# Both weight buffers of the experts and three of the four score stacks of the first attention in one memory

## The chip, the cores and the metric

The kernel runs on one core of a Trainium2 chip, as one launch. The metric is the device time of that launch in microseconds (us); lower is better. The core has five engines that run side by side and meet only at semaphores: TensorE (PE; its weight loads are shown apart as PEld), VectorE (DVE), ScalarE (ACT), GpSimd (POOL) and SyncE (SP), which issues nearly all DMA transfers. All tiles that the engines compute on lie in SBUF, 128 partitions wide; a tile's start is a byte address that is the same in every partition.

## The reference, cut to what matters

Two transformer layers on x of shape [16, 512, 256]. Layer 0: windowed attention with rotary positions, then a mixture of 8 experts of which each token takes 2. Layer 1: causal attention with xpos positions, then a product with a ternary weight.

```python
x = x + _L0_attn_ref(_layernorm(x), Wqkv, Wout)                  # 16 heads of 16, window 128
x = x + _L0_ffn_ref(_layernorm(x), Wr, br, Wl1, bl1, Wl2, bl2, biases_N)
x = x + _L1_attn_ref(_layernorm(x), Wq, bq, Wk, bk, Wv, bv, Wo, bo)   # causal
x = x + _L1_ffn_ref(_layernorm(x), weight)                       # ternary weight

# _L0_ffn_ref, per token: softmax over 8 scores, top 2, and
h = x @ Wl1[e] + bl1[e]            # 256 -> 2 * 512, both halves
y = (silu(h[:512]) * h[512:]) @ Wl2[e] + bl2[e]                  # 512 -> 256
# weighted sum of the two experts' y
```

## The kernel before, in words

The program has three stages, one after the other, with a barrier of all engines between them: `pipeline` for the first attention (its tiles show as `a_...` in the profile), `experts` (tiles `e_...`), and `pipeline` again for the second attention with the ternary product (`a_...` once more).

**pipeline** goes over the 16 sequences in turns. In turn i, PE makes the transposed scores of sequence i (step `T`, L1203, with a mask product L1080 behind them), ACT takes their exponentials (L672), PE multiplies them with the values (`PV`, L1221), and in the same turn PE makes the scores of sequence i+1 (step `S`, L1177) from which DVE takes each row's maximum (L941 in the first attention, L936 and L941 in the second). Sequence i+2 is projected and rotated (L1075, DVE L921 and L925, POOL L569 to L580), split into three bf16 parts, stored to DRAM (`store`, L473) and read back as stacks (`stack`, L483): `qst` and `kst`, each 98 partitions by 16 heads by 512 positions in bf16, 16,384 bytes in a partition. 96 of the partitions are the parts; the last two hold the negated maximum for q (L488) and ones for k (L440). There are two slots of each stack: sequence s uses `qst[s % 2]` and `kst[s % 2]`. The order of all steps is one list that every engine walks (`order`, sorted by position numbers in `turn`); semaphores are placed by hand, and no planner or pool decides anything. A stack's group g of slot s % 2 is written when the `T` steps of sequence s-2 with that group are done (wait on `t_done` ahead of L483).

**experts** goes over 39 steps: 32 of 512 rows and 7 of 256 rows. A step multiplies gathered rows with one expert's first weights (L1539, 48 matmuls), gates them on ACT and DVE, and multiplies with its second weights (L1555). Even steps use weight slot 0 and odd steps slot 1. A slot is `NW` = 3,072 fp32 columns twice (a rounded part and a rest), so 24,576 bytes in a partition; SP loads it in two transfers (L1380 of 2 MB, L1385 of 1 MB), two biases behind them (L1388, L1389). The weights of step 0 are loaded at the end of the first attention (`first_weights`, L1323) once all `T` steps of sequence 14, the last in slot 0, are done; those of step 1 are loaded in the experts' stage, behind the barrier (L1380).

**SBUF.** Tiles lie one behind the other in the order in which they are made. What `experts` makes ahead of its call of `pipeline` stays through the first attention; what it makes after the call takes the place of the attention's own tiles. `under` (L1313 of the code, `e_under` in the profile) is such a tile that stays: its bytes hold `qst[0]` and `kst[0]` of the first attention, and afterwards weight slot 0. `qst1` and `kst1` are tiles of the first attention, and weight slot 1 (`w1`, `e_w` in the profile) is a tile of the experts alone. The second attention has all four stacks as tiles of its own.

```python
under = sb("under", [P, H * T])                                      # L1313, ahead of the first attention
w = [under[:, 0:2 * NW].rearrange("p (l n) -> p l n", l=2)]          # L1314
w.append(sb("w1", [P, 2, NW]))                                       # L1334, behind it
```

Of the kernel before, what the change touches and what calls it, by code (L numbers as in the profile page):

```python
# [13 lines left out]
BF16 = mybir.dt.bfloat16  # L14
# [5 lines left out]
B, T, D = 16, 512, 256  # L20
P = 128
NT = T // P
KC = D // P
H, DH = 16, 16
# [14 lines left out]
AUG = ROWS + 2  # L39
# [90 lines left out]
def pipeline(nc, name, x_in, x_out, w_all, w_out, tables, biases, window, scale, consts, routed, mixed, ternary_w):  # L130
# [123 lines left out]
    with ctx:  # L254
        def sb(n, shape, dt=F32):
            return ctx.enter_context(nc.sbuf_tensor(f"{name}_{n}", shape, dt))
# [21 lines left out]
        ident = sb("ident", [P, P])  # L278
# [20 lines left out]
        parts = sb("parts", [P, 2, 3, 2, T], BF16)  # L299
        if routed:  # L300
            under = routed[-1][-1]
            qst, kst = ([under[0:AUG, a * H * T // 2:(a + 1) * H * T // 2].bitcast(BF16)
                         .rearrange("p (h t) -> p h t", h=H)] for a in range(2))
            qst.append(sb("qst1", [AUG, H, T], BF16))
            kst.append(sb("kst1", [AUG, H, T], BF16))
        else:
            qst = [sb(f"qst{i}", [AUG, H, T], BF16) for i in range(2)]
            kst = [sb(f"kst{i}", [AUG, H, T], BF16) for i in range(2)]
# [12 lines left out]
        if routed:  # L321
            xs, wr_d, br_d, bn_d, below_d, before_d, choice, ws_d, w1_d, w2_d, starts_d, kept = routed
            gate, place, expert, taken = choice
            rn, row, tile_tab, per_expert, shifts, scattered, padded, first_weights, under = kept
# [935 lines left out]
NW = KC * 2 * FF + FC * D  # L1260
# [27 lines left out]
def experts(nc, xs, ys, w1_d, b1_d, w2_d, b2_d, starts_d, ident_d, choice, yrow):  # L1288
# [10 lines left out]
    with ctx:  # L1299
        def sb(n, shape, dt=F32):  # L1300
            return ctx.enter_context(nc.sbuf_tensor(f"e_{n}", shape, dt))

        def sem(n):
            return ctx.enter_context(nc.semaphore(f"e_{n}"))
# [5 lines left out]
        shifts = sb("shifts", [P, 4, NE])  # L1310
        scattered = [sem(f"scattered{i}") for i in range(2)]
        padded = sem("padded")
        under = sb("under", [P, H * T])  # L1313
        w = [under[:, 0:2 * NW].rearrange("p (l n) -> p l n", l=2)]  # L1314
        b1 = [sb(f"b1{i}", [P, 2 * FC]) for i in range(2)]
        b2 = [sb(f"b2{i}", [P, D]) for i in range(2)]
        w1_loaded = [sem(f"w1_loaded{i}") for i in range(2)]
# [4 lines left out]
        def first_weights(sp, e):  # L1322
# [3 lines left out]
            sp.dma_start(b2[0][:, :], b2_d[e].partition_broadcast(P)).then_inc(b_loaded[0], 16)  # L1326

        pipeline(nc, *held["attention"], held["routed"] +
                 (ws_d, w1_d, w2_d, starts_d, (rn, row, tab, rows, shifts, scattered, padded, first_weights, under)), None, None)

        bank = [ctx.enter_context(nc.psum_tensor(f"e_bank{i}", [P, 512], F32)) for i in range(8)]
        AB, BB, YB, TB = bank[0:2], bank[2:4], bank[4:6], bank[6:8]
        ident = sb("ident", [P, P])
        w.append(sb("w1", [P, 2, NW]))  # L1334
        xg = sb("xg", [P, NT, D])
        xh = [sb(f"xh{i}", [P, KC, T], F32R) for i in range(2)]
        xl = [sb(f"xl{i}", [P, KC, T], F32R) for i in range(2)]
# [255 lines left out]
def ternary(nc, x_in, x_out, w_d, ident_d):  # L1593

    name, _, _, w_all, w_out, tables, biases, window, scale, consts = held["attention"]
    x1, ys = held["mixed"]
    pipeline(nc, name, x1, x_out, w_all, w_out, tables, biases, window, scale, consts, None,
             (ys,) + held["choice"], w_d)
# [105 lines left out]
```

How the kernel before makes its waits and increments, by code:

```python
        @block.sync  # L428
        def _(sp):
            if mixed:
                sp.dma_start(yrow[:, :, :], yrow_d).then_inc(index_loaded, 16)
                sp.dma_start(gate[:, :, :], gate_d).then_inc(index_loaded, 16)
            sp.dma_start(xt[0][:, :, :], x_in[0].rearrange("(t p) d -> p t d", p=P)).then_inc(x_loaded[0], 16)
            sp.dma_start(w_raw, w_all).then_inc(w_loaded, 16)
            sp.dma_start(ident[:, :], ident_d).then_inc(ident_loaded, 16)
            for dst, src in loads:
                sp.dma_start(dst, src).then_inc(const_loaded, 16)
            sp.wait_ge(ones_done, 1)
            for i in range(2):
                sp.dma_start(kst[i][ROWS:AUG, :, :], junk[0:2 * H, 0, :]).then_inc(ones_loaded, 16)
            for st in order:
                if st[0] == "fetch":
                    j = st[1]
                    e, c = divmod(j, NW // WCOLS)
                    src = w1_d[e][:, c, :] if c < KC else w2_d[e].rearrange("p c n -> p (c n)")
                    sp.wait_ge(ws_stored, 16 * j)
                    sp.dma_start(ws[:, 1, :], src).then_inc(ws_loaded, 16)
                elif st[0] == "keep":
                    j = st[1]
                    e, c = divmod(j, NW // WCOLS)
                    sp.wait_ge(rest_done, j + 1)
                    sp.dma_start(ws_d[e][:, :, c * WCOLS:(c + 1) * WCOLS], ws[:, :, :]).then_inc(ws_stored, 16)
                elif st[0] == "pads":
                    sp.wait_ge(counted_rows, 1)
```

## Time and profile before

| | before |
|---|---|
| median of 3 runs | 2888.07 us (2873.35, 2892.66, 2888.07) |
| the profiled execution | 2870.61 us, of it 2868.7 us from the first to the last instruction |
| PE busy | 2463.0 us, 86% of the span |
| DVE / ACT / POOL busy | 1714.3 / 1350.0 / 923.1 us |
| mean granted clock of TensorE | 0.943 of full speed |
| DMA | 490.19 MB, 171 GB/s over the span |

The page has one execution of the program: busy time by engine, the span in 40 slices, the DMA queues, the chain of work that ended last, and the costliest groups of instructions by line and tile. A group's row ends with the idle time of the engine ahead of it and with what ended that idle time. Names of tiles come without buffer numbers: `a_qst` is `qst1` in the first attention and both slots in the second.

### The profile page before, as it was taken

What the parts mean: (1) busy time and instruction counts of PE and PEld (TensorE: products, weight loads), DVE (VectorE), ACT (ScalarE), POOL (GpSimd) and SP (SyncE); (2) the same over time, 40 slices, a digit from 0 to 9 for tenths busy, and PEclk for the clock granted to TensorE, in tenths of its full rate; (3) what the DMA queues carried; (4) which work ended last, traced back from release to release, by engine and by line L of the source; (5) the groups of instructions that cost most, each with busy time, mean ns of one, the idle gap of its engine ahead of it and who ended that gap; (6) DMA issues with size and microseconds to landing.
All of it is one profiled execution on the core that took longest, in us unless ns stands there. A gap on an engine that the chain in (4) does not pass through costs nothing. (4 is left out here: it accounts for less than half of the span.)

```text
span 2868.7 us, 50929 instructions
## 1 busy us (share of the span) xinstructions
PE 2463.0 (86%) x17722; PEld 1682.5 (59%) x17722; DVE 1714.3 (60%) x5759; ACT 1350.0 (47%) x2419; POOL 923.1 (32%) x863
## 2 busy tenths in 40 slices
PE   3788888888889849999999982799999999998997
PEld 2455555555555528898998872455555555555553
DVE  3666676766667535444444434667676677666651
ACT  2455555555555423333333321255655555555654
POOL 2434555444553220000000015344443434444300
PEclk7899999999999969999999996799999999999998
DMA  4456555666545267877777745444455444444320
GB/s 134 152 185 212 185 181 183 205 213 190 176 156 170 75 205 250 285 267 263 267 280 265 252 146 173 119 119 143 127 146 145 134 119 118 124 135 141 117 62 15
DMA packets 259617, 490.19 MB, mean 171 GB/s; under 512 B 25609, under 2 KB 191113, under 8 KB 249417
## 3 DMA queue, kind: packets, MB, share of 16 engines
q1 hardware_dynamic: 241944, 435.23, 48.3%
q0 software_dynamic: 17456, 52.19, 5.4%
q8 instruction: 123, 2.02, 0.3%
q14 instruction: 94, 0.76, 0.1%
HBM read 299.65 MB, written 186.52 MB: 169 GB/s over the span
## 5 line engine op out<-in xcount | busy, mean ns | idle before, releaser
L672 ACT ACTIVATE a_pr<-a_bank 128x512 f32<-128x512 f32 (+1 forms) x1152 | 638.2, 573 | 571.2 <-PE a_bank L1080 500.6
L941 DVE CUSTOM_DVE_ANT_0 a_junk<-a_bank,a_smask 128x256 bf16<-128x256 f32 (+3 forms) x1536 | 652.1, 463 | 375.2 <-PE a_bank L1177 358.1
L1177 PE MATMUL a_bank<-a_kst,a_qst 96*128 96x256 bf16 (+3 forms) x1536 | 354.5, 297 | 76.5 <-DVE a_nmax L941 26.6
L1203 PE MATMUL a_bank<-a_qst,a_kst 98*128 98x256 bf16 (+3 forms) x1536 | 345.0, 292 | 43.0 <-ACT a_pr L672 25.2
L1221 PE MATMUL a_bank<-a_pr,a_va 128*32 128x256 f32 (+3 forms) x4096 | 350.7, 418 | 28.1 <-ACT a_pr L672 25.3
L1080 PE MATMUL a_bank<-a_mask,a_identb 128*128 128x512 bf16 (+2 forms) x1152 | 351.5, 305 | 0.0
L1177 PEld LDWEIGHTS a_bank<-a_kst,a_qst 96*128 96x128 bf16 x1536 | 127.5, 99 | 268.7 <-issue 84.1
L1426 POOL DMA_DIRECT2D results_dram<-e_yt x39 | 29.3, 751 | 619.2 <-DVE e_yt L1494 601.6
L1449 ACT ACTIVATE e_sa<-e_bank,e_b 128x512 f32<-128x512 f32 (+1 forms) x156 | 101.5, 651 | 255.9 <-PE e_bank L1539 236.0
L550 POOL DMA_INDIRECT xs<-e_rn,e_row x128 | 127.1, 993 | 294.8 <-DMA a_kst<-a_parts_dram 89.0
L1203 PEld LDWEIGHTS a_bank<-a_qst,a_kst 98*128 98x128 bf16 x1536 | 134.0, 99 | 143.7 <-ACT a_pr L672 72.9
L1506 DVE SCALAR_TENSOR_TENSOR e_gf<-e_bank,e_b,e_sa 128x512 f32<-128x512 f32 (+1 forms) x156 | 109.4, 701 | 164.8 <-ACT e_sa L1449 164.4
L1539 PE MATMUL e_bank<-e_xh,e_under 128*128 128x512 f32 x640 | 202.1, 397 | 1.4 <-DVE e_xl L1515 1.4
L936 DVE TENSOR_REDUCE a_nmax<-a_bank 128x2 f32<-128x512 f32 (+1 forms) x192 | 129.9, 684 | 97.1 <-PE a_bank L1080 97.1
L1221 PEld LDWEIGHTS a_bank<-a_pr,a_va 128*32 128x32 f32 x4096 | 85.7, 110 | 166.9 <-issue 108.4
L580 POOL TENSOR_TENSOR a_parts<-a_qk,a_parts 128x1024 bf16<-128x1024 f32 x64 | 136.6, 2134 | 80.5 <-ACT a_parts L647 80.4
L1510 DVE TENSOR_TENSOR e_gl<-e_gf,e_gh 128x512 fp32r<-128x512 f32 (+1 forms) x156 | 100.5, 644 | 103.5 <-ACT e_gh L1454 103.5
L1539 PE MATMUL e_bank<-e_xh,e_w 128*128 128x512 f32 (+1 forms) x608 | 161.1, 353 | 0.0
L1454 ACT CAST e_gh<-e_gf 128x512 fp32r<-128x512 f32 (+1 forms) x156 | 90.8, 582 | 142.0 <-DVE e_gf L1506 142.0
L576 POOL TENSOR_TENSOR a_qk<-a_qk,a_parts 128x1024 f32<-128x1024 f32 x64 | 136.7, 2136 | 39.8 <-ACT a_parts L644 39.5
L560 POOL DMA_INDIRECT a_yg<-results_dram,a_yrow x124 | 120.5, 972 | 73.4 <-DVE a_xt L779 45.2
L569 POOL TENSOR_TENSOR a_qk<-a_rt 128x512 f32<-128x512 f32 x64 | 81.8, 1279 | 178.1 <-DVE a_rt L921 115.5
(214 smaller groups left out, 5352.9 us busy)
## 6 DMA issues: line engine op xcount, KB each, us to landing
a_parts_dram<-a_parts SPq DMA_DIRECT2D x224, 256.0 KB
e_under<-ws_dram SPq DMA_DIRECT2D x20, 2048.0 KB, 9.0
e_w<-ws_dram SPq DMA_DIRECT2D x19, 2048.0 KB, 9.2
a_qst<-a_parts_dram SPq DMA_DIRECT2D x96, 384.0 KB, 7.6
a_kst<-a_parts_dram SPq DMA_DIRECT2D x96, 384.0 KB, 8.7
a_parts_dram<-a_parts SPq DMA_DIRECT2D x32, 768.0 KB
e_under<-a_parts_dram SPq DMA_DIRECT2D x64, 384.0 KB, 8.3
ws_dram<-a_ws SPq DMA_DIRECT2D x24, 1024.0 KB, 7.7
```

The lines of the kernel that those rows point to most:

```text
L550: pool.indirect_dma_start(xs, bass.IndirectOffsetOnAxis(ap=row[r % 2][:, k, t:t + 1], axis=0), rn[r % 2][:, t, :], None).then_inc(scattere ...
L560: pool.indirect_dma_start((xn if ahead else yg)[:, t, :], None, ys, bass.IndirectOffsetOnAxis(ap=yrow[:, k, m * NT + t:m * NT + t + 1], ax ...
L576: nc.gpsimd.tensor_tensor(qk[:, a], qk[:, a], parts[:, a, 0], ALU.subtract)\
L580: nc.gpsimd.tensor_tensor(parts[:, a, 2], qk[:, a], parts[:, a, 1], ALU.subtract)\
L672: nc.scalar.activation(pr[b][:, h:h + per, :], TB_[at % 2][:, 0:per * w].rearrange("p (h w) -> p h w", h=per), ACT.Exp, scale=scale).then_ ...
L936: last = nc.vector.tensor_reduce(nmax[:, qb, g * HG + h:g * HG + h + per], SB_[at % 2][:, 0:per * w].rearrange("p (h w) -> p h w", h=per), ...
L941: last = nc.vector.tensor_tensor_reduce(junk[:, at % 2, j * w:(j + 1) * w], SB_[at % 2][:, j * w:(j + 1) * w], smask[:, T - w:T], scale=-1 ...
L1080: return nc.tensor.matmul(out, identb[:, :], rhs, start=False, stop=True, skip_group_check=True)
L1177: last = nc.tensor.matmul(out[:, j * w:(j + 1) * w], q[0:ROWS, hh, qb * P:(qb + 1) * P], k[0:ROWS, hh, k0:k0 + w], start=not whole or j == ...
L1203: nc.tensor.matmul(out[:, j * w:(j + 1) * w], k[0:AUG, hh, b * P:(b + 1) * P], q[0:AUG, hh, q0:q0 + w], start=(j == 0), stop=False, skip_g ...
L1221: last = nc.tensor.matmul(PVB[32 * j:32 * (j + 1), q0:q0 + w], va[i % 2][:, b, (g * HG + j) * VW:(g * HG + j) * VW + 32], pr[b][:, j, :], ...
L1539: last = nc.tensor.matmul(out[:, 0:s.columns], first(s.slot, low)[:, kc, col:col + P], x[s.slot][:, kc, 0:s.columns], start=(p == 0), stop ...
```

## The change

`under` grows from 8,192 to 12,288 fp32 columns. Weight slot 1 becomes its second half and is no tile of its own any more. In the first attention `qst[1]` becomes the third 16,384 bytes of `under`; `kst[1]` stays a tile. The experts' `ident` tile is made ahead of `under` instead of behind the attention. The second attention is not touched.

```diff
         if routed:
             under = routed[-1][-1]
-            qst, kst = ([under[0:AUG, a * H * T // 2:(a + 1) * H * T // 2].bitcast(BF16)
-                         .rearrange("p (h t) -> p h t", h=H)] for a in range(2))
-            qst.append(sb("qst1", [AUG, H, T], BF16))
-            kst.append(sb("kst1", [AUG, H, T], BF16))
+            parts_of = [under[0:AUG, n * H * T // 2:(n + 1) * H * T // 2].bitcast(BF16)
+                        .rearrange("p (h t) -> p h t", h=H) for n in range(3)]
+            qst = [parts_of[0], parts_of[2]]
+            kst = [parts_of[1], sb("kst1", [AUG, H, T], BF16)]
...
-        under = sb("under", [P, H * T])
-        w = [under[:, 0:2 * NW].rearrange("p (l n) -> p l n", l=2)]
+        ident = sb("ident", [P, P])
+        under = sb("under", [P, 4 * NW])
+        w = [under[:, i * 2 * NW:(i + 1) * 2 * NW].rearrange("p (l n) -> p l n", l=2) for i in range(2)]
...
-        ident = sb("ident", [P, P])
-        w.append(sb("w1", [P, 2, NW]))
```

Both kernels make 25,716 instructions (loops counted once), one for one the same in kind, shape, engine and semaphores; only addresses in SBUF differ. Where the tiles start, in bytes within a partition, as both programs were built:

| tiles | before | after | moved by |
|---|---|---|---|
| `under`: `qst[0]`, `kst[0]`, weight slot 0 | 27,328 | 27,840 | +512 |
| first attention, `qst[1]` | 144,416 | 60,608 | (into `under`) |
| first attention, `kst[1]` and all tiles behind it | 160,800 and up | 161,312 and up | +512 |
| first attention, all tiles ahead of the stacks (`wh` to `parts`), and the experts' biases | 60,096 and up | 76,992 and up | +16,896 |
| weight slot 1 | 62,720 | 52,416 | (into `under`) |
| experts, `xg` and all tiles behind it | 87,296 and up | 79,104 and up | -8,192 |
| experts, `ident` | 62,208 | 27,328 | -34,880 |
| second attention, all tiles | | | 0 |

All these distances but `ident`'s are multiples of 256 bytes. `qst[1]` starts 32 bytes past a multiple of 256 before and 192 past one after; weight slot 1 starts on a multiple of 256 before and 192 past one after. `under` starts 192 past one in both.

SP's queue in the first attention where the stacks of sequence 1 are loaded (L483) and the maxima of sequence 0 are put under its q stack (L488), before; each row has its line, its tiles and in brackets the semaphores that it waits for:

```order
38 L483 DMA a_qst<-a_parts_dram 96x2048 [waits a0_t_done,a0_parts_stored1,a0_parts_stored0]
39 L483 DMA a_kst<-a_parts_dram 96x2048
40 L483 DMA a_qst<-a_parts_dram 96x2048 [waits a0_t_done]
41 L483 DMA a_kst<-a_parts_dram 96x2048
42 L488 DMA e_under<-a_nmt 2x8x512 [waits a0_flip_free]
43 L483 DMA a_qst<-a_parts_dram 96x2048 [waits a0_t_done]
```

The same place of the same queue after the change:

```order
38 L483 DMA e_under<-a_parts_dram 96x2048 [waits a0_t_done,a0_parts_stored1,a0_parts_stored0]
39 L483 DMA a_kst<-a_parts_dram 96x2048
40 L483 DMA e_under<-a_parts_dram 96x2048 [waits a0_t_done]
41 L483 DMA a_kst<-a_parts_dram 96x2048
42 L488 DMA e_under<-a_nmt 2x8x512 [waits a0_flip_free]
43 L483 DMA e_under<-a_parts_dram 96x2048 [waits a0_t_done]
```

Nothing moved: the same transfers stand in the same places behind the same semaphores, and where the row named `a_qst` it names `e_under`.

## Rows read from the trace of the kernel before

**Rows 1.** The page: span, busy time by engine, and the chain by engine.
```profile
span 2868.7 us, 50929 instructions
...
PE 2463.0 (86%) x17722; PEld 1682.5 (59%) x17722; DVE 1714.3 (60%) x5759; ACT 1350.0 (47%) x2419; POOL 923.1 (32%) x863
...
PE 18%; DVE 6%; POOL 5%; ACT 4%; issue 4%; DMA 2%; SPq 0%; DVEq 0%; POOLq 0%; ACTq 0%
```

**Rows 2.** Windows: stretch, its length, busy time (instructions), granted clock, DMA share, GB/s.
```profile
0.00:1022.80 1022.80, 839.96 (x6750) 538.93 (x6750) 656.43 (x3160) 512.85 (x897) 439.46 (x398) 0.93 0.54 170
...
1080.00:1710.00 630.00, 626.47 (x3848) 560.95 (x3849) 306.99 (x485) 224.73 (x389) 28.54 (x38) 0.99 0.74 256
...
1770.00:2868.00 1098.00, 964.90 (x6984) 557.35 (x6984) 702.72 (x1974) 598.10 (x1112) 403.21 (x370) 0.96 0.41 120
```

**Rows 3.** PE's waits: line, what ended them, us in total, times, the longest.
```profile
PE e_bank L1577 <- DMA e_xg<-xs: 26.9, 1, 26.9
...
PE a_bank L1177 <- DMA e_under<-a_parts_dram: 20.4, 1, 20.4
PE a_bank L1203 <- DMA e_under<-a_nmt: 19.3, 8, 3.8
PE a_bank L1203 <- DMA a_qst<-a_nmt: 16.9, 7, 6.0
```

**Rows 4.** First attention, PE on the slot 0 stacks: ns minimum/median/maximum, first and last start.
```profile
L1177 PE MATMUL a_bank<-e_under x512: 216/273/421, 55.3 to 930.7; 96*128 96x256 bf16 x128, 96*128 96x128 bf16 x43
L1203 PE MATMUL a_bank<-e_under x512: 217/271/421, 103.5 to 979.6; 98*128 98x256 bf16 x128, 98*128 98x128 bf16 x43
```

**Rows 5.** First attention, PE on the slot 1 stacks, the same columns.
```profile
L1177 PE MATMUL a_bank<-a_kst,a_qst x512: 217/272/421, 105.1 to 980.2; 96*128 96x256 bf16 x128, 96*128 96x128 bf16 x43
L1203 PE MATMUL a_bank<-a_qst,a_kst x512: 217/272/421, 158.6 to 1021.0; 98*128 98x256 bf16 x128, 98*128 98x128 bf16 x43
```

**Rows 6.** DMA issues: tile, count, KB, median us to landing (stacks: first attention alone).
```profile
e_under<-ws_dram SPq DMA_DIRECT2D x20, 2048.0 KB, 9.0
e_w<-ws_dram SPq DMA_DIRECT2D x19, 2048.0 KB, 9.2
...
e_under<-a_parts_dram SPq DMA_DIRECT2D x64, 384.0 KB, 8.3
...
a_qst<-a_parts_dram SPq DMA_DIRECT2D x32, 384.0 KB, 7.2
a_kst<-a_parts_dram SPq DMA_DIRECT2D x32, 384.0 KB, 8.0
```

**Rows 7.** Groups by form, experts: count, busy us, mean ns, idle before.
```profile
L1539 PE MATMUL e_bank<-e_xh,e_under 128*128 128x512 f32 x640 | 202.1, 397 | 1.4 <-DVE e_xl L1515 1.4
...
L1539 PE MATMUL e_bank<-e_xh,e_w 128*128 128x512 f32 x384 | 119.5, 392 | 0.0
...
L1555 PE MATMUL e_bank<-e_w,e_gh 128*128 128x256 f32 x496 | 92.1, 283 | 0.0
L1555 PE MATMUL e_bank<-e_under,e_gl 128*128 128x256 f32 x320 | 90.1, 281 | 0.0
```

**Rows 8.** Timeline, PE in L1539, one matmul in three: slot 1, then slot 0.
```profile
1679.22 0.39 PE L1539 MATMUL e_bank<-e_xl,e_w 128*128 128x512 f32 x1
...
1683.30 0.39 PE L1539 MATMUL e_bank<-e_xl,e_w 128*128 128x512 f32 x1
...
1683.98 0.39 PE L1539 MATMUL e_bank<-e_xl,e_under 128*128 128x512 f32 x1
...
1688.79 0.39 PE L1539 MATMUL e_bank<-e_xl,e_under 128*128 128x512 f32 x1
```

**Rows 9.** Timeline, PE in L1555, one matmul in three: slot 1, then slot 0.
```profile
1654.96 0.27 PE L1555 MATMUL e_bank<-e_w,e_gl 128*128 128x256 f32 x1
...
1660.34 0.28 PE L1555 MATMUL e_bank<-e_w,e_gl 128*128 128x256 f32 x1
...
1672.55 0.28 PE L1555 MATMUL e_bank<-e_under,e_gl 128*128 128x256 f32 x1
...
1677.85 0.28 PE L1555 MATMUL e_bank<-e_under,e_gl 128*128 128x256 f32 x1
```

**Rows 10.** POOL's L576, first attention, then second: ns minimum/median/maximum.
```profile
L576 POOL TENSOR_TENSOR a_qk<-a_qk,a_parts x32: 2113/2134/2147, 30.1 to 915.1; 128x1024 f32<-128x1024 f32 x32
...
L576 POOL TENSOR_TENSOR a_qk<-a_qk,a_parts x32: 2121/2132/2160, 1759.5 to 2716.2; 128x1024 f32<-128x1024 f32 x32
```

**Rows 11.** SP's queue, the loads of weight slot 1: first and last start.
```profile
L1380 SPq DMA_DIRECT2D e_w<-ws_dram x19: 559/574/597, 1081.7 to 1648.8; - x19
```

## The prediction

> **What bounds the kernel now.** I read the page first, then the windows by stage, then PE's waits. The program is on the device for 2870.61 us, of which 2868.7 are the span; PE is busy in 2463.0 of them, and it has the largest part of the chain that ended last, 18% against DVE's 6% [rows 1]. By stage [rows 2]: in the first attention, 0 to 1022.8 us, PE is busy for 839.96 us (82%) at a granted clock of 0.93 of full speed; in the experts, 1080 to 1710 us, for 626.47 of 630 us; in the second attention, 1770 to 2868 us, for 964.90 of 1098 us. So the experts' stage is PE from end to end, and both attentions are PE with short waits for DVE and ACT. The reader should see in those rows that a change can only be worth something in one of two ways: PE gets other matmuls or slower ones, or PE waits for something else. PE's waits that have to do with the memories at hand are few [rows 3]: 20.4 us once for the first stack of all, 19.3 us in 8 waits for the maxima of slot 0 and 16.9 us in 7 for those of slot 1. None of its larger waits is for weights: the only wait for a transfer in the experts is the 26.9 us for the first gathered rows.
>
> **What the change removes, adds and moves.** No instruction goes, none comes, and none changes its place; the piece of SP's queue shown above has the same semaphores in the same rows, and the same holds for every other row of the five queues. So the sum has no term of work. What is left is where 49,152 bytes of a partition lie, and every term is a question of the form: does the same instruction take another time at another address? I go through the tiles by what touches them.
>
> *PE on the first attention's stacks.* 1,024 matmuls read `qst[1]` (512 in L1177, 512 in L1203). The trace of before has the very comparison, since slot 0 lay in `under` already: 273 and 271 ns at the median there [rows 4], 272 and 272 ns in slot 1 [rows 5]. The difference is +1 and -1 ns; 512 times each is 0.5 us up and 0.5 us down. Term: 0. Bounds: -0.5 to +0.5 us.
>
> *PE on weight slot 1.* Here the slots do differ a little. The mean of a 512-column matmul is 397 ns from `under` and 392 ns from `e_w` [rows 7]. Pipelined matmuls are better read by their pace. In L1539, six triples of slot 1 take 1683.30 - 1679.22 = 4.08 us, or 680 ns each, and seven triples of slot 0 take 1688.79 - 1683.98 = 4.81 us, or 687 ns [rows 8]. In L1555 it is the other way round: 15 triples of slot 1 take 5.38 us, 359 ns each, and 15 of slot 0 take 5.30 us, 353 ns [rows 9]. The trace does not tell whether the address of the weights makes this, or that of the other operand (`xh`, `gh`, which have two slots of their own), or the program's code. If the weights' address does it, slot 1 in `under` takes slot 0's pace: its L1539 has 304 triples (608 + 304 matmuls), and at most 7 ns on each are +2.1 us; its L1555 has 248, and 6 ns less on each are -1.5 us. Together +0.6 us. If it is the other operands' address, all of them move by the same 8,192 bytes and keep their distances, and the likeliest is 0. The far bounds: every step takes the slower pace of both lines, +2.1 us in L1539 of slot 1 and 6 ns on 320 triples of slot 0 in L1555, +1.9 us, so +4 us; or every step the faster one, -7 ns on 320 triples of slot 0 in L1539 and -1.5 us, so -3.7 us. I take 0, since the two known differences have opposite signs.
>
> *Transfers into the stacks and the weights.* Into `under`, which starts 192 bytes past a multiple of 256, the 2 MB of weights land 9.0 us after issue; into slot 1, which starts on such a multiple before the change, 9.2 us after [rows 6]. For the stacks it is 8.3 us in `under` for q and k together, and 7.2 and 8.0 us for q and k of slot 1, 7.6 on the mean. If `qst[1]` landed like a stack in `under`, its 32 loads would land up to 1.1 us later. In the steady turns this lies under the previous turn's scores: the wait for a stack in the first attention is the 20.4 us at its start, in slot 0, whose place moves by 512 bytes only. Term 0; if the cover were gone, 1.1 us once in each of 8 sequences is 9 us, and that is the outer bound above.
> The Trainium skill, page "DMA: Bandwidth & Descriptors", section "How a descriptor splits into AXI transactions", says that a descriptor which does not start on a 256-byte boundary pays for the bytes below its start. By it weight slot 1, which leaves such a boundary, would cost some 2% more beats on its 8 KB rows, which on the 9.2 us of its row is an estimate of 0.2 us a load, and 4 us over 19 loads if none were hidden. The rows of before speak against it here: the start off the boundary lands in 9.0 us and the start on it in 9.2.
>
> *All other tiles.* They move by multiples of 256 bytes. For them I have the same instruction at two places: POOL's subtraction L576 takes 2134 ns at the median in the first attention and 2132 ns in the second, whose tiles lie elsewhere [rows 10]. 2 ns on 32 of them is 0.06 us. The other moved tiles get the same answer, 0.
>
> *A wait by sharing.* The second half of `under` (slot 1) lies over `kst[0]` and `qst[1]`. A wait for their last reader would be needed if the weights were loaded early; they are not. The last matmul on `qst[1]` starts at 1021.0 us [rows 5] and the first load of slot 1 at 1081.7 us, behind the barrier [rows 11]. It was there before and stays.
>
> The sum: 2870.6 + 0 for the profiled execution, with bounds of -4 and +5 (pace and stacks' matmuls), +14 with the transfers uncovered. That execution is 17.5 us under the median of the three runs, and they differ among themselves by 19 us, far more than any term. The four times known (2870.6, 2873.4, 2888.1, 2892.7) have a mean of 2881 us; I predict that, since the changed kernel draws from the same spread.
>
> **The rivals.**
> *The pace of the experts' matmuls follows the addresses.* For it: a real difference of 7 ns and 6 ns between slots. Against it: opposite signs. It gives 2881 - 4 to 2881 + 4 us, which can't be told from no change; I count it with the first case.
> *Slower: the shared memory itself costs.* The mechanism would be that PE's reads of `qst[1]` and slot 1 suffer now that they lie next to what DMA fills: slot 0's stacks are written while PE reads slot 1's, and weights of one slot while PE reads the other. It decides from +29 us (1%) on. 1,024 matmuls in the attention and 1,656 in the experts would each need +11 ns (29 us over 2,680). The rows speak against it: slot 0's groups are written in `under` one by one while PE reads its other groups there, and the median in it is 272 ns as elsewhere [rows 4, 5]. At three times the largest difference seen, 21 ns for a triple, it is 7 ns a matmul, +19 us: 2900 us. For the full case, 2915 us. Chance 0.03.
> *Faster: a placement effect in the 16,896 bytes by which most of the attention's tiles move.* For it, nothing but that the trace shows no such move for DVE and ACT in one stage; the point is again 29 us, 2.8% of the first attention's 1022.8. Against it: the 2 ns of L576. It would give 2850 us. Chance 0.03.
> *The change frees time by freeing memory.* It frees 8,192 bytes in the experts' stage, and no tile and no extra buffer takes them. 2881 us, within the first case.
>
> **How the numbers follow.** No change, small paces and transfers included: 0.94, at 2881 us. Slower 0.03, faster 0.03. The range takes the lowest known time less the 4 us of pace, 2866, and the highest plus 4, 2897, and a few us more on either side because four executions show only part of a spread: 2863 to 2901 us. The outer cases are left out of it. About 1% is what a measurement of this kernel can tell from no change, and the chances of faster, same and slower by over 1% are those of the three cases.
>
> **What would show it right or wrong.** In the profile after: 50,929 instructions or within a few records of it, stages of 1023, 57, 630, 60 and 1098 us each to within 5 us; L1177 and L1203 in `under` at 271 to 273 ns; in the experts, slot 1's triples at 680 or 687 ns in L1539 and 359 or 353 in L1555, which tells whether the weights' address makes the pace; the 2 MB loads at 9.0 to 9.2 us. I am wrong if a stage is 10 us longer or shorter at the same granted clock, if a matmul of the stacks has another median, or if PE waits for a transfer into `under` where it did not. What would also make the number wrong, though not the reasons, is a spread of executions that is wider than the four known ones.

## The result

| | before | after |
|---|---|---|
| median of 22 runs | 2886.42 us (2873.35 to 2895.45) | 2872.63 us (2865.18 to 2881.12) |
| ratio | 1 | 0.9959, 95% interval 0.9947 to 0.9971 |
| the profiled execution | 2870.61 us, span 2868.7 | 2869.44 us, span 2867.2 |
| PE from the first to the last matmul of L1539/L1555 (L1538/L1554 after) | 630.0 us | 621.1 us |

The changed kernel is faster by 0.41%, some 12 us, with the same instructions in the same order. That is inside the range of the forecast and inside "within 1%", but the interval leaves out 1 and a second comparison (e4, below) finds it again, so it is a real difference, and I had forecast none. The two profiled executions hardly differ in their spans, since that of before was one of its fastest; so the stages have to be compared, and not the spans.

The windows by stage of after, as in [rows 2]: length, busy PE, PEld, DVE, ACT, POOL, granted clock, DMA share, GB/s.

```profile
0.00:1034.00 1034.00, 836.74 (x6621) 542.57 (x6730) 654.85 (x3153) 512.73 (x894) 439.03 (x398) 0.92 0.54 168
...
1093.20:1714.30 621.10, 618.09 (x3852) 551.54 (x3852) 306.48 (x484) 224.09 (x389) 28.52 (x38) 1.00 0.75 260
...
1776.00:2867.00 1091.00, 953.92 (x6920) 554.93 (x6984) 702.78 (x1974) 597.12 (x1112) 401.78 (x369) 0.96 0.42 120
```

The same window of before, cut at the same two matmuls:

```profile
1080.60:1710.60 630.00, 627.06 (x3852) 561.45 (x3852) 306.45 (x484) 224.13 (x389) 28.54 (x38) 0.99 0.74 256
```

3,852 matmuls and 3,852 weight loads in both, and PE idle for 3 us of the stage in both: 9 us less in PE itself, with DVE's, ACT's and POOL's busy time unchanged to 0.1 us. Some of these 9 us are clock, by an estimate 3 (half of the time that before spends longer at the lower level): PE starts the stage at the lower of its two clock levels for 5.6 us in before and 3.1 us in after, and only before has 3.4 us of it at the end, where its last 16 triples take 448 ns each (granted clock 0.92 from 1690 us on) against 353 in after (1.00). The first attention was 11 us longer in this execution of after than in that of before; a second execution of the very same kernel (e4, below) reached the experts 21 us earlier than this one, so this says nothing about the change.

By form, the rows of after that answer to [rows 7] (both slots are `e_under` now):

```profile
L1538 PE MATMUL e_bank<-e_xh,e_under 128*128 128x512 f32 x1024 | 321.4, 395 | 1.4 <-DVE e_xl L1514 1.4
...
L1554 PE MATMUL e_bank<-e_under,e_gl 128*128 128x256 f32 x568 | 157.1, 277 | 0.0
```

L1554 has a mean of 277 ns where before had 281 (slot 0) and 283 (slot 1) [rows 7]. The pace in the timeline of after, as in [rows 8, 9], shows every third matmul, the one that reads `gl` or `xl`, first in L1554, then in L1538. A triple is three matmuls in a row, one of each kind, and its time is that from one such matmul to the next.

```profile
1679.04 0.28 PE L1554 MATMUL e_bank<-e_under,e_gl 128*128 128x256 f32 x1
...
1683.12 0.28 PE L1554 MATMUL e_bank<-e_under,e_gl 128*128 128x256 f32 x1
1683.80 0.39 PE L1538 MATMUL e_bank<-e_xl,e_under 128*128 128x512 f32 x1
...
1693.41 0.39 PE L1538 MATMUL e_bank<-e_xl,e_under 128*128 128x512 f32 x1
```

Twelve triples of 256 columns take 4.08 us, 340 ns each; before had 353 in slot 0 and 359 in slot 1 [rows 9]. Fourteen triples of 512 columns take 9.61 us, 686 ns each, and both slots have this pace (687 in every longer block); before had 687 and 680 [rows 8]. So L1554 is faster in **both** slots, though slot 0 has moved by 512 bytes only.

Read step by step through the whole stage, the trace of before has a pattern that I had missed. Its experts go in rounds of four steps (the fourth has 256 rows), and L1555's pace in them is 353, 360, 341 and 357 ns a triple, in every one of the seven rounds, and 353 and 360 in turn in the last eleven steps but the very last, which ran at a lower clock. The third step of a round, slot 0 in before:

```profile
1502.77 0.28 PE L1555 MATMUL e_bank<-e_under,e_gl 128*128 128x256 f32 x1
...
1507.88 0.28 PE L1555 MATMUL e_bank<-e_under,e_gl 128*128 128x256 f32 x1
```

Fifteen triples in 5.11 us, 341 ns: the same slot, the same addresses as the 353 of [rows 9], another pace. In after every step has 340 to 342 but two: the third, at 353, and the last, at 353 behind a wait of 2.9 us.

The transfers and the stacks are as before: 9.1 us to landing for all 39 loads of 2 MB, against 9.0 and 9.2 [rows 6]; 272 and 272 ns at the median on the stacks that moved, against 272 and 272 [rows 5]. Medians of durations can hide a pace, as they did for L1554, so I also took the time from one start to the next within these blocks: 113 ns at the median for the 256-column matmuls of L1177 and of L1203 on slot 1, in both kernels.

```profile
e_under<-ws_dram SPq DMA_DIRECT2D x39, 2048.0 KB, 9.1
```
```profile
L1177 PE MATMUL a_bank<-a_kst,e_under x512: 217/272/421, 105.8 to 992.8; 96*128 96x256 bf16 x128, 96*128 96x128 bf16 x43
L1203 PE MATMUL a_bank<-e_under,a_kst x512: 217/272/421, 160.8 to 1034.2; 98*128 98x256 bf16 x128, 98*128 98x128 bf16 x43
```

### The profile page after: what moved, and what is told of

The parts are those of the page before. It is cut to its first block and busy times, and to the rows that moved or that the text cites. A ratio compares the mean times of both kernels' runs of the same rounds, so it can differ in the third digit from the quotient of the medians.

```text
span 2867.2 us, 50756 instructions
## 1 busy us (share of the span) xinstructions
PE 2441.9 (85%) x17549; PEld 1675.3 (58%) x17722; DVE 1713.9 (60%) x5759; ACT 1350.5 (47%) x2419; POOL 922.0 (32%) x863
## 5 line engine op out<-in xcount | busy, mean ns | idle before, releaser
L1538 PE MATMUL e_bank<-e_xh,e_under 128*128 128x512 f32 (+1 forms) x1248 | 361.3, 374 | 1.4 <-DVE e_xl L1514 1.4
L1177 PE MATMUL a_bank<-a_kst,a_qst 96*128 96x128 bf16 (+3 forms) x1024 | 264.1, 310 | 59.9 <-DVE a_nmax L936 23.8
L1080 PE MATMUL a_bank<-a_mask,a_identb 128*128 128x128 bf16 (+2 forms) x979 | 282.7, 289 | 0.0
L1203 PE MATMUL a_bank<-a_qst,a_kst 98*128 98x512 bf16 (+3 forms) x1024 | 253.8, 303 | 25.9 <-ACT a_pr L672 25.1
L1538 PEld LDWEIGHTS e_bank<-e_xh,e_under 128*128 128x128 f32 x1248 | 222.2, 189 | 40.7 <-DVE e_xl L1514 1.8
L1538 PE MATMUL e_bank<-e_xl,e_under 128*128 128x512 f32 (+1 forms) x624 | 233.2, 374 | 0.0
L1177 PEld LDWEIGHTS a_bank<-a_kst,a_qst 96*128 96x128 bf16 x1024 | 85.8, 98 | 204.8 <-DVE a_nmax L936 62.8
L1554 PE MATMUL e_bank<-e_under,e_gh 128*128 128x256 f32 x1136 | 200.7, 277 | 2.9 <-DVE e_gl L1509 2.9
L1554 PEld LDWEIGHTS e_bank<-e_under,e_gh 128*128 128x128 f32 x1136 | 174.2, 188 | 4.5 <-DVE e_gl L1509 3.4
L1554 PE MATMUL e_bank<-e_under,e_gl 128*128 128x256 f32 x568 | 157.1, 277 | 0.0
```

The lines of the kernel that those rows point to most:

```text
L1080: return nc.tensor.matmul(out, identb[:, :], rhs, start=False, stop=True, skip_group_check=True)
L1177: last = nc.tensor.matmul(out[:, j * w:(j + 1) * w], q[0:ROWS, hh, qb * P:(qb + 1) * P], k[0:ROWS, hh, k0:k0 + w], start=not whole or j == ...
L1203: nc.tensor.matmul(out[:, j * w:(j + 1) * w], k[0:AUG, hh, b * P:(b + 1) * P], q[0:AUG, hh, q0:q0 + w], start=(j == 0), stop=False, skip_g ...
L1538: last = nc.tensor.matmul(out[:, 0:s.columns], first(s.slot, low)[:, kc, col:col + P], x[s.slot][:, kc, 0:s.columns], start=(p == 0), stop ...
L1554: last = nc.tensor.matmul(YB[n][:, (t % k) * D:(t % k + 1) * D], x[s.slot][:, f, t * P:(t + 1) * P], second(s.slot, low)[:, f, :], start=( ...
```

## The experiments

There were three theories at the start. **A**: the pace follows the address of the other operands (`xh`, `xl`, `gh`, `gl`), which moved by 8,192 bytes. **B**: it follows the address of the weights. **C**: it has nothing to do with data but with where PE's instructions lie, and any new program draws it anew. "Pace" is the time of a triple (one matmul of each of the three products of high and rest parts) in the timeline. "Stage" is the window from the first to the last matmul of the experts. Its first and last few us depend on the clock that is granted there, which differs by 1 to 3 us between executions of one kernel; so I also give the **steady part**, the time from the 121st to the 1081st of the 1,192 triples, each taken by its matmul on `xl` or `gl`.

**e1: the kernel before, unchanged.**

> The kernel before, unchanged. It asks whether the pace of PE in the experts' stage is a property of the program. In the trace of before, triples of 256-column matmuls in L1555 take 353 ns in the first of every four steps, 360 in the second, 341 in the third and 357 in the fourth, and the stage takes 630 us. If the pace comes from anything the program fixes (addresses of tiles, place of the instructions), it is the same here to 1 ns, and the stage is 630 us to within 1 us. If it is drawn anew with each load or each execution, another pattern shows. Time: 0.998 to 1.002 of before either way.

Measured: the same pattern, 353, 360, 341 and 357 to 360 ns, in every round; stage 630.8 us; steady part 500.5 us against 500.3 in the first trace; ratio 0.9990 (0.9977 to 1.0003). The pace is a property of the program. The ratio of the kernel to itself comes out 3 us below 1, with an interval that holds 1 and reaches 7 us below it: a comparison of this size can be off by a few us.

**e4: the kernel after, unchanged.**

> The kernel after, unchanged. Its trace showed 341 ns a triple in L1554 in all steps but two of the first four (353 and 354), and 621 us for the experts' stage. If the program fixes the pace, the same steps show the same figures, those two among them, and the ratio to before is 0.995 to 0.997. If the pace is drawn with each load, the two slow steps lie elsewhere or are gone.

Measured: ratio 0.9960 (0.9942 to 0.9977), stage 624.3 us, steady part 495.4 against 494.8, and of the first four steps the third alone at 353. The expectation names two slow steps; read again, the first trace too has one in L1554 there, and the second block at 353 is that of 256 columns in L1538 right behind it. The result repeats in a second comparison, at another level of both (2855.37 against 2869.01 us).

**e2: the other operands back where they were.**

```diff
+        sb("pad", [P, 2048])
         xg = sb("xg", [P, NT, D])
```

> The kernel after, with 8,192 unused bytes ahead of the experts' xg, so that xg, xh, xl, gf, gh, gl and yt start where they did before the change; weights and the first attention stay as after. Theory A (the address of the matmuls' other operands sets the pace): the experts' stage goes from 621 back to about 630 us, L1554 from 341 to 353 and 360 ns a triple, ratio to before 0.998 to 1.000. Theory B (the address of the weights sets it): the stage stays at 621 us and the ratio at 0.996. Theory C (the place of PE's instructions sets it, not data): also 621 us or, since the program is built anew, any other pattern, but not just the old one.

Measured: 341 ns and 687 ns stay, stage 624.0 us, steady part 494.9 us; ratio 0.9975 (0.9960 to 0.9989). The ratio lies between what A and B expect and its interval reaches both; the pace and the steady part decide. A in this form is out: 8,192 bytes do nothing to the pace.

**e3: four more instructions on PE.**

```diff
                         elif f == 0:
-                            pe.wait_ge(const_loaded, 16)
+                            for _ in range(8):
+                                pe.wait_ge(const_loaded, 16)
```

(Eight waits make four instructions more.)

> The kernel before, with four more semaphore instructions on PE at the start of the experts' stage (waits for what has long been reached; they cost well under 1 us). All tiles stay where they were; every later instruction of PE stands four places further on. Theories A and B (data addresses): L1555 keeps 353, 360, 341 and 357 ns a triple, and the stage 630 us. Theory C (place of the instructions): the pattern changes, with the stage anywhere between 620 and 635 us.

Measured: 353, 360, 341 and 357 as before, stage 629.6 us, steady part 500.5 us, ratio 0.9998 (0.9981 to 1.0014). C is out for a shift by four instructions; other shifts were not tried, but the next run leaves no need for it.

**f1: weight slot 1 moved by 192 bytes, in the kernel before.**

```diff
+        sb("pad0", [P, 48])
         w.append(sb("w1", [P, 2, NW]))
+        sb("pad1", [P, 16])
```

> The kernel before with weight slot 1 moved by 192 bytes, from 62,720 (a multiple of 256) to 62,912 (192 past one, as slot 0 lies); tiles behind it move by 256, nothing else. Theory B1 (where the weights start within 256 bytes sets the pace of PE in the experts): slot 1's 512-column triples go from 680 to 687 ns, its 256-column triples in L1555 and L1539 from 360 to 341, slot 0's from 353 to 341, the stage from 629 to about 622 us, ratio to before 0.996 to 0.998. Theory B2 (the region in which slot 1 lies, 62 to 87 thousand against 52 to 77 thousand, or its lying next to slot 0): no pace changes, stage 629 us. Theory B3 (the 512 bytes by which slot 0 moved, or the ident tile): also no change here.

Measured: ratio 0.9964 (0.9950 to 0.9978; 5 executions), which can't be told from the whole of the result, without a shared memory, a moved `qst` or a moved `ident`. Stage 623.5 us, steady part 494.8 us. By form:

```profile
L1557 PE MATMUL e_bank<-e_under,e_gl 128*128 128x256 f32 x320 | 89.3, 279 | 0.0
...
L1557 PE MATMUL e_bank<-e_w,e_gl 128*128 128x256 f32 x248 | 68.6, 277 | 0.0
L1541 PE MATMUL e_bank<-e_xh,e_w 128*128 128x256 f32 x224 | 40.1, 280 | 0.0
```

Slot 1 goes from 283 to 277 ns, as B1 says, and slot 0, which has not moved at all, from 281 to 279, its pace from 353 to 341. The gain comes without what B2 and B3 need; f2, next, has what they need and no gain. Both are out.

**f2: both slots on a multiple of 256, in the kernel after.**

```diff
-        under = sb("under", [P, 4 * NW])
-        w = [under[:, i * 2 * NW:(i + 1) * 2 * NW]...
+        under = sb("under", [P, 4 * NW + 64])
+        w = [under[:, 16 + i * 2 * NW:16 + (i + 1) * 2 * NW]...
```

> The kernel after with both weight slots moved 64 bytes on within the shared memory, so that both start on a multiple of 256 (27,904 and 52,480); the stacks stay where they are in it, tiles behind it move by 256. Theory B1: both slots show what slot 1 showed before, 680 ns for three matmuls of 512 columns and about 360 for three of 256, the stage goes from 622 to about 631 us (568 triples by 19 ns more is 10.8, 512 by 7 ns less is 3.6, 112 of 256 columns in L1538 by 19 ns is 2.1), ratio to before 0.999 to 1.003. Theories B2 and B3: the stage stays at 622 us and the ratio at 0.996.

Measured: ratio 0.9998 (0.9983 to 1.0012), stage 631.1 us, steady part 502.4 us. The timeline:

```profile
1663.53 0.28 PE L1554 MATMUL e_bank<-e_under,e_gl 128*128 128x256 f32 x1
...
1668.93 0.28 PE L1554 MATMUL e_bank<-e_under,e_gl 128*128 128x256 f32 x1
```

That is 5.40 us for 15 triples, 360 ns, now in both slots and in all steps; L1538 at 681 to 682 in its blocks of twelve. This run also has everything else that the change does, the first attention's part with it, and the gain is gone: with 64 bytes it is given back.

**f4: both slots 128 past a multiple of 256.**

```diff
+        under = sb("under", [P, 4 * NW + 64])
+        w = [under[:, 48 + i * 2 * NW:48 + (i + 1) * 2 * NW]...
```

> The kernel after with both weight slots moved 192 bytes on, so that both start 128 bytes past a multiple of 256 (28,032 and 52,608). It asks for the grain of the effect. If 64-byte steps matter (an odd multiple of 64 is the fast place), this is like starting on a multiple of 256: 680 and 360 ns, stage about 631 us. If only a multiple of 256 is slow, 687 and 341 ns stay and the stage is 622 us. Theories B2 and B3: 622 us.

Measured: a fourth pattern that I had not expected in either case: 696 to 702 ns for 512 columns, and 356 to 360 for the 256 of L1554, stage 640.1 us, steady part 507.4, ratio 1.0017 (1.0000 to 1.0034). So it is not "on a multiple of 256 or not".

**f3: first weights on a multiple of 256, second ones 192 past one.**

```diff
-        under = sb("under", [P, 4 * NW])
+        under = sb("under", [P, 4 * NW + 320])
+        w = [under[:, 16 + i * 2 * (NW + 64):16 + (i + 1) * 2 * (NW + 64)]...
+        N2 = KC * 2 * FF + 48      # second weights: N2 to N2 + FC * D
...
+        ident = sb("ident", [P, P])      # behind the experts' other tiles
```

> The kernel after with a gap between a slot's first and second weights, so that the first ones (L1538) start on a multiple of 256 in both slots and the second ones (L1554) 192 bytes past one. The ident tile stands behind the experts' other tiles again. Theory B1: L1538's 512-column triples at 680 ns, L1554's at 341 unless the pace of L1538 carries over (then 353, as slot 0 had it before); the 112 triples of 256 columns in L1538 at 360. Stage 622 - 3.6 + 2.1 = 620.5 us without the carrying over, and up to 6.8 us more with it. Theories B2 and B3: 622 us.

Measured: L1539 (its line in this kernel) at 680 ns, L1555 at 353 in three steps of a round and at 341 in the third, as slot 0 had it before; stage 627.0 us, steady part 497.6, ratio 0.9974 (0.9964 to 0.9985). The third step of the first round, and then a step of the last eleven:

```profile
1152.32 0.28 PE L1555 MATMUL e_bank<-e_under,e_gl 128*128 128x256 f32 x1
...
1157.43 0.28 PE L1555 MATMUL e_bank<-e_under,e_gl 128*128 128x256 f32 x1
...
1653.20 0.28 PE L1555 MATMUL e_bank<-e_under,e_gl 128*128 128x256 f32 x1
...
1658.51 0.28 PE L1555 MATMUL e_bank<-e_under,e_gl 128*128 128x256 f32 x1
```

Fifteen triples take 5.11 us and 5.31 us, 341 and 354 ns each. The pace carries over: the matmuls of L1555 have the addresses' remainders of after, and run at 353 where L1539 ahead of them ran at 680 for 512 columns, and at 341 where L1539 ahead of them had 256 columns. By this the 341 of the third step of before is explained too, and why slot 0 became faster in f1 without being moved: its L1555 is preceded by slot 1's L1539.

That carrying over is not the whole rule. In after the third step of every round has the same instructions, the same addresses and the same kind of block ahead of it, and L1554 runs there at 353 ns in the first round and at 340 in the six others:

```profile
1144.88 0.28 PE L1554 MATMUL e_bank<-e_under,e_gl 128*128 128x256 f32 x1
...
1150.18 0.28 PE L1554 MATMUL e_bank<-e_under,e_gl 128*128 128x256 f32 x1
```

Fifteen triples in 5.30 us are 353 ns. The four triples of L1538 right ahead took 340 ns there and 353 in the later rounds. What decides between the two was not found.

**Whose address, or whose distance?** The patterns so far (weights at 192, at 0 and at 128 past a multiple of 256, and at 0 and 192 mixed), with all other operands on such a multiple, leave two readings. **W**: the weights' own start within 256 bytes sets the pace. **R**: the distance between a matmul's two operands within 256 bytes does.

**g1: the other operands 64 bytes on, weights as in after.**

```diff
+        sb("pad", [P, 16])
         xg = sb("xg", [P, NT, D])
```

> The kernel after with 64 unused bytes ahead of the experts' xg: weights still start 192 past a multiple of 256, but xg, xh, xl, gh and gl now 64 past one instead of on one. Theory R (the distance of a matmul's two operands within 256 bytes sets the pace): weights minus other operand was 192 and becomes 128, so the paces of the run with the weights at 128 come back, 697 ns for three matmuls of 512 columns and 356 to 360 for three of 256 in L1554, the stage at 638 us, ratio 1.001 to 1.002. Theory W (the weights' own start sets it): 687 and 341 ns and 622 us stay, ratio 0.996.

Measured: the weights have not moved, and the pattern of f4 is back, 695 to 701 ns and 355 to 360; stage 639.6 us, steady part 507.0 us (f4: 507.4), ratio 1.0032 (1.0013 to 1.0051).

```profile
1670.54 0.28 PE L1555 MATMUL e_bank<-e_under,e_gl 128*128 128x256 f32 x1
...
1675.88 0.28 PE L1555 MATMUL e_bank<-e_under,e_gl 128*128 128x256 f32 x1
```

5.34 us for 15 triples, 356 ns.

**g2: weights on a multiple of 256 (the slow place of f2), the other operands 64 past one.**

```diff
+        under = sb("under", [P, 4 * NW + 64])
+        w = [under[:, 16 + i * 2 * NW:16 + (i + 1) * 2 * NW]...
...
+        sb("pad", [P, 16])
         xg = sb("xg", [P, NT, D])
```

> The kernel after with the weights on a multiple of 256 (the place that gave 680 and 360 ns) and xg to gl 64 past one. Theory R: the distance is 192 again, so 687 and 341 ns, stage 622 us, ratio 0.996. Theory W: 680 and 360 ns, stage 630 us, ratio 1.000.

Measured: the pattern of after, 341 and 687, the third step of the first round at 353 with it; stage 623.4 us, steady part 494.7 us, ratio 0.9971 (0.9952 to 0.9989).

```profile
1673.10 0.28 PE L1555 MATMUL e_bank<-e_under,e_gl 128*128 128x256 f32 x1
...
1677.18 0.28 PE L1555 MATMUL e_bank<-e_under,e_gl 128*128 128x256 f32 x1
```

4.08 us for 12 triples, 340 ns. R holds in both runs and W in neither.

**g3: the distance that was missing.**

```diff
+        under = sb("under", [P, 4 * NW + 64])
+        w = [under[:, 32 + i * 2 * NW:32 + (i + 1) * 2 * NW]...
```

> The kernel after with both weight slots 64 past a multiple of 256 and the other operands on one: the one distance in steps of 64 that no run has shown. Neither theory says what it gives. The first weights are the stationary operand in L1538 and the second weights the moving one in L1554, so at 64 the two lines change parts of what 192 gives; if only the size of the distance counted and not its sign, 64 would be as 192: 687 and 341 ns and 622 us. I expect 340 to 360 in L1554 and 680 to 700 in L1538, a stage of 615 to 638 us.

Measured: 353 ns in all of L1554, 700 in L1538, 340 to 353 for its 256 columns; stage 635.9 us, steady part 505.4 us, ratio 1.0012 (0.9992 to 1.0032). The sign of the distance counts: 64 is not 192.

**g4: the rule put to use in the first attention.**

```diff
+        if routed:
+            sb("pad0", [P, 8])
         xh = sb("xh", [P, KC, T], F32R)
         xl = sb("xl", [P, KC, T], F32R)
+        if routed:
+            sb("pad1", [P, 56])
```

> The kernel after with xh and xl of the first attention 32 bytes further on (124,480, that is 64 past a multiple of 256; they were 32 past one), tiles behind them 256 further on. The value product in L1075 (stationary xh or xl, moving wh or wl, 256 columns) then has a distance of 192 as in the experts and in the second attention, instead of 224. Theory R: its triples go from 354 ns to about 341 in the first attention; 256 triples by 13 ns are 3.3 us of work, of which what is not hidden by waits shows, so a ratio to before of 0.995 against 0.996 for after. Theory W: no change, since wh and wl start on a multiple of 256 as before; 354 ns and 0.996.

The value product of the first attention in after, and then in g4, one matmul in three:

```profile
519.70 0.28 PE L1075 MATMUL a_bank<-a_wl,a_xh 128*128 128x256 f32 x1
...
521.47 0.28 PE L1075 MATMUL a_bank<-a_wl,a_xh 128*128 128x256 f32 x1
```
```profile
518.31 0.28 PE L1079 MATMUL a_bank<-a_wl,a_xh 128*128 128x256 f32 x1
...
520.35 0.28 PE L1079 MATMUL a_bank<-a_wl,a_xh 128*128 128x256 f32 x1
```

Five triples in 1.77 us are 354 ns, six in 2.04 us are 340: R again, in another stage and for other tiles. (These are one stretch of each trace; over the whole first attention the matmuls of this line start 117 to 121 ns apart at the median in after and 114 in g4.) Over the launch the ratio to before is 0.9957 (0.9938 to 0.9976) against 0.9959 for after: the gain of at most 3.3 us can't be told from none, and g4 beats the kernel before but is not shown to beat the changed one.

All places together, sorted by the weights' start minus the other operand's, modulo 256 (for L1538 the weights are stationary, for L1554 moving). "At times" are the third step of the first round and the last step, as in after; the steady part given for f2 is that of f2 alone:

| distance | runs | L1538, 512 columns | L1554, 256 columns | steady part |
|---|---|---|---|---|
| 0 | f2; slot 1 of before | 680 to 682 ns | 360 ns | 502.4 us |
| 64 | g3 | 698 to 701 | 353 | 505.4 |
| 128 | f4, g1 | 695 to 702 | 355 to 360 | 507.4, 507.0 |
| 192 | after, e2, e4, f1, g2, g4 | 687 | 341, at times 353 | 494.7 to 495.4 |
| 0 in L1538, 192 in L1554 | f3 | 680 | 353; 341 in the third step | 497.6 |
| 192 in slot 0, 0 in slot 1 | before, e1, e3 | 687 and 680 | 353 and 341; 360 and 357 | 500.3 to 500.5 |

## Why the prediction was right or wrong

**The time and "no change": right, by luck in part.** 2872.63 us lies in 2863 to 2901, and 0.9959 within 1%. But 2881 was a mean of four executions of before, whose own median over 22 runs is 2886.4; I was 5 us low on that and 8 us high on the changed kernel.

**No instruction moves: right.** 3,852 matmuls in the stage, the same waits. PE's waits for weights stay at none, and the wait ahead of the first stack is 20.3 us (20.4 in [rows 3]).

**The stacks of the first attention: right.** 272 and 272 ns, and 113 ns from start to start in both kernels, though the distance of the two operands of slot 1 went from 0 to 160 bytes within 256. **The transfers: right.** 9.1 us. The Trainium skill's rule on descriptors that start off a 256-byte boundary ("DMA: Bandwidth & Descriptors", "How a descriptor splits into AXI transactions") would have made slot 1's loads longer, by the prediction's estimate 0.2 us. The section says it of what a transaction reads, and the start that moved here is where the loads write. The traces could not show so little either: the median of the 2 MB loads is 9.0 us in f2, with both slots on a boundary, and 9.1 in after and 8.4 in g1, with both 192 past one. What starts on a boundary of 256 matters here, but to PE.

**The pace of the experts' matmuls: the step that failed.** The mechanism stood there, as a rival counted with "no change"; its size was wrong, with "-4 to +4 us" as bounds where the steady part alone moved by 5.5 us and the whole stage by 6 to 9. Three things were wrong in that term. First, "its L1539 has 304 triples" at 7 ns: 112 of them are of 256 columns and go from 359 to 340 and 353 ns instead. Second, I took 353 ns for slot 0's own pace, from one block, and so the pace that slot 1 would take over. Slot 0 had 341 in every third step of a round; it was 353 only behind slot 1's 512-column matmuls. One block of each slot was too small a sample of a stage with 39. Third, "every step the faster one" of the paces in two blocks was no bound, since those were not the fastest paces. And the working asked only whose address sets the pace; that the distance between the two operands might was not among its cases. Worked out again from the paces by step: 16 triples in a full step and 8 in a half one; L1555 of slot 0, 13 steps by 16 by 12 ns is -2.5 us; of slot 1, 12 steps by 16 by 19 ns is -3.6 us, and 7 half steps by 8 by 16 ns is -0.9; L1539 of 256 columns, 112 by some 14 ns is -1.6; of 512 columns, 192 by 7 ns is +1.3. The sum is -7.3 us. The steady part, four fifths of the stage, says -5.5 us, which agrees. The ratio says -11.8 us with an interval of 3.5 to either side, so 1 to 8 us of it are not in this sum.

Where the rest is stays open. It is not in the first attention's part of the change as far as f2 can tell, which has that part and comes to 0.9998; and f1, which lacks it, comes to 0.9964. e1, the kernel against itself, is 0.9990, so a few us of the rest can be the comparison's own. The sum of -7.3 us is a ratio of 0.9975, which lies in the intervals of e2, e4, f1, g2 and g4, the other runs with after's distance, though four of these five come out lower (0.9957 to 0.9971).

**"If it is the other operands' address, all of them move by the same 8,192 bytes": right as far as it goes** (e2), and of no use: what counts is the distance to the weights within 256 bytes, which 64 bytes change (g1) and 8,192 don't.

**The slower rival** (PE reads suffering next to what DMA fills) **was wrong**: the slots lie side by side in after, f2, f3, f4 and g2 alike, with and without the gain. Its full case of 2915 us doesn't follow from its own working either, since 2881 + 29 is 2910. **The faster rival** looked in the wrong stage.

**What was to show it wrong**: "a stage 10 us longer or shorter at the same granted clock" is nearly what came, 8.9 us in the experts at 0.99 and 1.00. It came in the first attention too, 11 us longer at 0.92 against 0.93. The expected stages of the two attentions, to within 5 us, were a bad check: two executions of after reach the experts 21 us apart.

## What to carry to other kernels

Where a stage is PE from end to end, a change that "only moves tiles" needs a forecast too: compare the pace of the same matmuls over all blocks of the stage, not the median of their durations and not one block, and look at where both operands start. In this kernel the place of two operands to each other within 256 bytes is worth up to 2.6% of such a stage (494.7 against 507.4 us of its steady part), and a pad of 64 to 192 bytes sets it. A difference of 0.4% in a launch that wanders by 0.7% was traced to its cause by the stage's pace and steady part, which repeat to 0.15%, and not by the totals; the stage's whole window is less sharp, 621.1 and 624.3 us for one kernel, because of the clock at its ends.

## What the runs showed of the hardware

- TensorE's pace on float32r matmuls depends on the distance between the starts of its moving and its stationary operand in a partition, modulo 256 bytes. For 256 columns, 341 ns for three at a distance (moving less stationary) of 192, 353 at 64, 360 at 0, 356 to 360 at 128 (L1554), and 354 at 224 and 340 at 192 in the first attention's value product. The 256-column triples of L1538 fit less well: 340 and 353 ns, in blocks of four or eight, at 64 (after) and at 192 (g3) alike, and 355 to 360 at 0 (f2). For 512 columns in L1538, 680 ns at 0, 687 at 64, 697 at 128, 700 at 192. All at the full granted clock. That 256 and not 512 is the period rests on slot 1 of before and f2, where the weights start 24,576 and 51,456 bytes ahead of `xg`, an odd multiple of 256 apart, and the paces are 360 and 680 to 682 ns in both. Only steps of 64 bytes, and one of 32, were tried. The bf16 matmuls of 256 columns on slot 1's stacks start 113 ns apart at a distance of 0 (before) and of 160 (after), so they show no such effect.
- The Trainium skill ("SBUF — State Buffer", "Who interferes with whom") gives PE two read ports, one for the moving operand and one for the weight loads, that are independent of each other. The pace follows the distance of the two operands (g1, g2), which independent ports would not make one expect; whether it is the ports, the memory behind them or something else that depends on that distance, no run here tells.
- A block of matmuls can keep a pace that the block ahead of it set: with the same remainders of its addresses, L1555 of f3 runs at 353 ns behind a 512-column block at 680 and at 341 behind a 256-column block at 360, without drifting within its 16 triples. But after has 353 in the third step of its first round and 340 in that of the later ones, with equal addresses and equal blocks ahead. Why was not found.
- The 2 MB loads show no difference between a start in SBUF on a multiple of 256 and 192 past one that is larger than their spread: 9.2 us (before, slot 1) and 9.0 (f2) on one, 9.0 (before, slot 0), 9.1 (after) and 8.4 (g1) past one.
